# Taking the transposition of the first normalisation off TensorE: four square transposes on VectorE and sixteen on-chip transfers, one tile ahead

## The chip, the cores and the metric

The kernel runs on one core of one Trainium2 chip. The metric is the device time in microseconds (us); less is better. Every engine has a queue of its own: TensorE (PE, matrix products), VectorE (DVE), ScalarE (ACT), GpSimd (POOL), and SyncE (SP), which here issues all the transfers (DMAs). An engine works through its instructions in order, and waits on semaphores that others raise.

## What is computed

One decoder layer in fp32 on x of shape (4, 1024, 512), with a context of (4, 64, 512) and an integer mask:

```python
x = x + self_attention(layernorm(x))             # one head, causal inside blocks of 128 rows
x = x + cross_attention(layernorm(x), context)   # 16 heads of 32, 64 keys, silu instead of softmax
x = x + ffn(layernorm(x))                        # 512 -> 2048 (gelu) -> 512

qkv = z @ W_qkv; scores = blk(q) @ blk(k).T * 512**-0.5; p = softmax(causal(scores))
out = (p @ blk(v)) @ W_out.T + b_out
attn = silu(where(mask == 0, -1e9, q @ k.T * 32**-0.5)); out = (attn @ v) @ Wo.T
```

## The kernel before

The 4096 rows of x are taken as eight tiles of 512 rows (`TILES`), each four blocks of 128 rows (`NB`). An activation `z` of a tile is held twice over: in rows (`zn`, 128 rows on the partitions, 512 features along them), and transposed (`zT`, features on the partitions in four chunks of 128, `EC`, and the 512 rows of the tile along them), since TensorE contracts over partitions. To keep fp32 accuracy on a faster format, each operand is split into a high and a low part (`_hi`, `_lo`); `product` (L49 to L52) makes each product out of three matmuls.

There are three stages, each a block of its own, between which all engines wait for each other:

1. **Setup** (L279 to L423). The weights come in as 32 pieces of 256 KB (`CHUNKS`) through eight buffers `raw(n)`, which lie in `resid`; SP reloads a buffer once `split_lo` says that it is used. ACT makes the high part of each (`split_high`, L303), DVE the low part (`split_low`, L331). PE folds W_q W_k^T into `wqk` and W_v W_out into `wvo` (`fold`, 48 matmuls each, behind nine warm-up matmuls on zeros, L402), and projects the values of the four batches, which DVE takes over with their bias (L366). DVE also makes the statistics and the rows `zn` of tile 0; PE transposes them with 16 matmuls against the identity (`transposed_chunks`, L163).
2. **Attention** (L484 to about L1030). `pipeline` runs a step for each tile a: `step(0, None, 0)`, `step(1, 0, 1)`, then two steps to a loop pass, and `last_step`. A step does the self-attention of tile a and, interleaved with it, the cross-attention of tile b = a - 1. The order within it is written out by hand, for each engine. On PE: four query products (`queries`, 48 matmuls), the 16 transposes of `zn` for tile a (L163) into four PSUM banks, cross scores of heads 0 to 7 (`cross_scores`, L871 and L873, 8 matmuls), `y` = `wqk` z (48 matmuls), values, self scores (L922, L924), and so on up to the transposes for the second normalisation (L146) and the last share of the output projection.
3. **Feed-forward** (about L1035 to L1230), where PE alternates between the two products of a tile. The transposed rows of the next tile are made there by DVE alone, with 16 instructions on squares of 32x32 (L1173) for each tile.

Around the change, on DVE at the start of a step, `start_step` aggregates the statistics of tile a (L722), then makes `kb_lo` (L730, four instructions, waiting for ACT's `kb_hi`) and the rows `zn` of tile a (L140, four). For b = 0 the rows come before `kb_lo`. Then come `q_low` (L703, two for each of four chunks), `chunk_low` (L172, the low part of `zT`, four), the mask (L734), `values_low` (L740, four), and `mask_scores` (L711) for heads 0 to 7. On ACT: `keys_high` (L605), `q_high` (L610), `chunk_high` (L168, the high part of `zT`). The statistics of tile a + 1 are taken in step a from `x_in` (`next_stats`, L248), which SP loads (L240) after the first residual has used its former rows.

```python
for i in range(NB):                                             # L163, transposed_chunks
    last = pe.transpose(bank[first_bank + c][:, cols(i)], zn[:, i, cols(c)], ident[:, :])
...
pe.wait_ge(z1T_lo, EC * a + m + 1)                              # in the step, before product (m, 0)
```

## Time and profile before

| | |
|---|---|
| median of 3 runs | 1264.19 us (1264.07 to 1264.53) |
| the profiled execution's own time | 1264.23 us |
| its span | 1261.8 us |
| PE busy | 1249.1 us, 99% of the span |
| DVE busy | 662.7 us, 53% |
| ACT busy | 487.2 us, 39% |
| POOL busy | 243.7 us, 19% |
| TensorE clock granted | full speed in all 40 slices |
| setup, attention, feed-forward begin on PE at | 1.73, 43.17, 561.87 us |

The span is what the profiler records between the first and the last instruction; 2.4 us lie around it. A matmul is pipelined: it is listed with 389 ns while the next one starts 227 ns after it, so the pace is read from the starts. "Idle before <- X" names what ended the idle time in front of an instruction.

### The profile page before, as it was taken

What the parts mean: (1) busy time and instruction counts of PE and PEld (TensorE: products, weight loads), DVE (VectorE), ACT (ScalarE), POOL (GpSimd) and SP (SyncE); (2) the same over time, 40 slices, a digit from 0 to 9 for tenths busy, and PEclk for the clock granted to TensorE, in tenths of its full rate; (3) what the DMA queues carried; (4) which work ended last, traced back from release to release, by engine and by line L of the source; (5) the groups of instructions that cost most, each with busy time, mean ns of one, the idle gap of its engine ahead of it and who ended that gap; (6) DMA issues with size and microseconds to landing.
All of it is one profiled execution on the core that took longest, in us unless ns stands there. A gap on an engine that the chain in (4) does not pass through costs nothing.

```text
span 1261.8 us, 15612 instructions
## 1 busy us (share of the span) xinstructions
PE 1249.1 (99%) x5785; PEld 1040.3 (82%) x5785; DVE 662.7 (53%) x1210; ACT 487.2 (39%) x888; POOL 243.7 (19%) x225
## 2 busy tenths in 40 slices
PE   9989999999999999999999999999999999999998
PEld 7878888888888888878888888888888888888887
DVE  7476868686868686865733333434424333434211
ACT  6246555555555555564322232222222322223221
POOL 2303232323232323258502001001001010010000
PEclk9999999999999999999999999999999999999999
DMA  8220202020202020316110010010100100100000
GB/s 296 88 63 13 76 14 75 13 76 12 75 12 75 12 75 12 125 46 220 52 67 1 1 67 1 1 66 0 51 15 0 66 0 0 66 0 0 34 1 34
DMA packets 40486, 60.04 MB, mean 48 GB/s; under 512 B 4224, under 2 KB 14464, under 8 KB 40448
## 3 DMA queue, kind: packets, MB, share of 16 engines
q1 hardware_dynamic: 40448, 59.53, 14.2%
q8 instruction: 24, 0.39, 0.1%
q14 instruction: 14, 0.11, 0.0%
HBM read 41.17 MB, written 18.35 MB: 47 GB/s over the span
## 4 chain that ended last, share of the span: by engine, by line
PE 55%; DVE 0%; issue 0%; DVEq 0%
PE bank L50 18%; PE bank L52 18%; PE bank L51 18%; DVE resid L1186 0%; DVEq L1185 0%
## 5 line engine op out<-in xcount | busy, mean ns | idle before, releaser
L1176 DVE TENSOR_TENSOR hid_lo<-gelu_out,hid_hi 128x512 fp32r<-128x512 f32 x128 | 97.5, 762 | 405.8 <-ACT gelu_out L1140 405.8
L50 PE MATMUL bank<-zT,w_parts 128*128 128x512 f32 x768 | 299.1, 389 | 3.4 <-DVE zT L155 1.8
L52 PE MATMUL bank<-zT,w_parts 128*128 128x512 f32 x768 | 298.8, 389 | 0.0
L51 PE MATMUL bank<-zT,w_parts 128*128 128x512 f32 x768 | 298.8, 389 | 0.0
L1136 ACT ACTIVATE hid_hi<-bank,small 128x512 fp32r<-128x512 f32 x128 | 88.3, 690 | 498.8 <-PE bank L52 498.8
L50 PE MATMUL bank<-w2p_hi,hid_lo 128*128 128x512 f32 x512 | 199.2, 389 | 0.0
L51 PE MATMUL bank<-w2p_lo,hid_hi 128*128 128x512 f32 x512 | 199.2, 389 | 0.0
L52 PE MATMUL bank<-w2p_hi,hid_hi 128*128 128x512 f32 x512 | 199.2, 389 | 0.0
L50 PEld LDWEIGHTS bank<-zT,w_parts 128*128 128x128 f32 x768 | 144.2, 188 | 34.4 <-issue 2.3
L51 PEld LDWEIGHTS bank<-zT,w_parts 128*128 128x128 f32 x768 | 144.2, 188 | 29.9
L52 PEld LDWEIGHTS bank<-zT,w_parts 128*128 128x128 f32 x768 | 144.1, 188 | 29.8
L554 POOL TENSOR_TENSOR attn_lo<-act_in,attn_hi 128x512 fp32r<-128x512 f32 x64 | 81.6, 1296 | 225.2 <-ACT act_in L599 225.2
L52 PEld LDWEIGHTS bank<-w2p_hi,hid_hi 128*128 128x128 f32 x512 | 96.2, 188 | 20.0
L51 PEld LDWEIGHTS bank<-w2p_lo,hid_hi 128*128 128x128 f32 x512 | 96.0, 188 | 20.0
L50 PEld LDWEIGHTS bank<-w2p_hi,hid_lo 128*128 128x128 f32 x512 | 96.1, 188 | 19.9
L133 POOL TENSOR_SCALAR ve<-mv 128x4 f32<-128x4 f32 x24 | 5.8, 240 | 500.4 <-DVE mv L128 351.0
L1140 ACT ACTIVATE gelu_out<-bank,small 128x512 f32<-128x512 f32 x128 | 87.3, 682 | 0.0
L1173 DVE STREAM_TRANSPOSE z_cols<-zn 32x512 f32<-32x512 f32 x112 | 78.7, 703 | 4.2
L1100 POOL TENSOR_TENSOR resid<-resid,b_row 128x512 f32<-128x512 f32 x32 | 45.2, 1442 | 116.2 <-DVE zn L140 116.2
L691 DVE TENSOR_TENSOR yv_lo<-bank,yv_hi 128x512 fp32r<-128x512 f32 x64 | 42.6, 686 | 39.2 <-ACT yv_hi L586 30.3
L598 ACT ACTIVATE attn_hi<-act_in 128x512 fp32r<-128x512 f32 x64 | 40.0, 625 | 31.4 <-DVE act_in L711 30.6
L50 PE MATMUL bank<-w_parts,zT 128*128 128x512 f32 x128 | 51.2, 400 | 0.0
(142 smaller groups left out, 1808.8 us busy)
## 6 DMA issues: line engine op xcount, KB each, us to landing
x_in<-in_x SPq DMA_DIRECT2D x32, 256.0 KB, 3.5
x_dram<-resid SPq DMA_DIRECT2D x32, 256.0 KB, 2.1
w_raw<-in_w SPq DMA_DIRECT2D x32, 256.0 KB, 3.3
resid<-x_dram SPq DMA_DIRECT2D x32, 256.0 KB, 3.8
out_dram<-resid SPq DMA_DIRECT2D x32, 256.0 KB, 2.1
resid<-in_wqkvT SPq DMA_DIRECT2D x12, 256.0 KB, 5.2
mask_i<-in_mask SPq DMA_DIRECT2D x16, 128.0 KB, 2.7
values_now<-values_dram SPq DMA_DIRECT2D x8, 256.0 KB, 2.8
```

What stands on the lines that cost most here:

```text
L50: pe.matmul(out_ap, lhs[1], rhs[0], start=start, stop=False)
L51: pe.matmul(out_ap, lhs[0], rhs[1], start=False, stop=False)
L52: return pe.matmul(out_ap, lhs[0], rhs[0], start=False, stop=stop)
L133: pool.tensor_scalar(ve[:, :], mv[:, :, 1], LN_EPS, None, ALU.add).then_inc(ln[2], 1)
L554: pool.tensor_tensor(attn[1][:, j % 4, :], act_in[:, j % 3, :], f(attn[0][:, j % 4, :]), ALU.subtract).then_inc(attn_lo, 1)
L598: act.activation(attn[0][:, j % 4, :], act_in[:, j % 3, :], ACT.Silu)
L691: dve.tensor_tensor(hl[1][:, m, :], bank[from_bank][:, :], f(hl[0][:, m, :]), ALU.subtract).then_inc(made, 1)
L1100: pool.tensor_tensor(resid[:, slot, i, :], resid[:, slot, i, :], b2_row[:, :], ALU.add).then_inc(x2_biased, 1)
L1136: act.activation(hid[0][:, c % 4, :], bank[4 + c % 3][:, :], ACT.Gelu, bias=b1_col[:, c:c + 1])
L1140: act.activation(gelu_out[:, c % 2, :], bank[4 + c % 3][:, :], ACT.Gelu, bias=b1_col[:, c:c + 1]).then_inc(hid_full, 1)
L1173: dve.transpose(*squares(TURNS_AT_ONCE * (c - FIRST_TURN) + n)).then_inc(z3_turned, 1)
L1176: dve.tensor_tensor(hid[1][:, c % 4, :], gelu_out[:, c % 2, :], f(hid[0][:, c % 4, :]), ALU.subtract).then_inc(hid_lo, 1)
```

## The change

For the tiles 1 to 7 the rows of the first normalisation are made and transposed one step earlier, with no work on PE:

- SP loads x of tile a + 2 in step a into `ahead`, which lies in the memory of the raw feed-forward weights (`raws`); tile 1 is loaded in the setup, behind `x_in` and ahead of four small loads and the weight pieces 12 and on. DVE takes its statistics there (`stats_ahead`, `aggregate`).
- At the start of step a, DVE makes the rows of tile a + 1 (`rows_ahead`), and later in the step transposes them with four instructions on 128 partitions (`turn`), which turn each 32x32 square in its place, into the same memory.
- SP then moves the squares between the four groups of 32 partitions with sixteen DMAs of 64 KB into a new buffer `z1_cols`, and waits for them before it loads tile a + 2.
- In step a + 1 ACT and DVE make the high and low parts of `zT` from `z1_cols` (`z1_high`, `z1_low`) in place of the PSUM banks, the first of them ahead of the fourth query chunk. PE no longer transposes there; its `y` products go to banks 0 to 3, and the other banks are dealt out anew.
- In the setup, `fold` runs the high-by-high matmuls of a piece before the others, waiting only for the high parts; one warm-up matmul fewer, and the first memset is halved. DVE gets the statistics of tile 1 ahead of the values (L366 before).
- GpSimd adds the bias to `x_in` before it does its low parts, and makes the reciprocal deviation of tile a + 2 at the end of step a.

```diff
@@ setup, sync @@
                                 for i in range(NB):
                                     load_x(sp, 0, i)
+                                load_ahead(sp, 1)
@@ setup, vector @@
                         for n in range(20, WO_CHUNK):
                             split_low(n)
+                        stats_ahead(dve, 1, range(NB))
+                        aggregate(dve, 1, mv1, ln1)
                         dve.wait_ge(bias_loaded, 64)
@@ setup, tensor: fold @@
+                                pe.wait_ge(split_hi, n + 2)
+                                for m in range(EC):
+                                    pe.matmul(bank[banks + m][:, :], part[0][:, n % PARTS, cols(m)],
+                                              part[0][:, (n + 1) % PARTS, :], start=c == 0, stop=False)
                                 pe.wait_ge(split_lo, n + 2)
...
@@ attention, sync @@
+                            if more(a):
+                                sp.wait_ge(z1_turned, NB * (a + 1))
...
+                                    sp.wait_ge(z1T_lo, EC * (a + 1))
+                                for r in range(QUADS):
+                                    for q in range(QUADS):
+                                        sp.dma_start(
+                                            z1_cols[cols(q, SQUARE), :, :].rearrange(
+                                                "f c (r n) -> f c r n", r=QUADS)[:, :, r, :],
+                                            raws[cols(r, SQUARE), 0:NB, :].rearrange(
+                                                "f c (q n) -> f c q n", q=QUADS)[:, :, q, :]
+                                            ).then_inc(z1_moved, 16)
+                            if twice_more(a):
+                                sp.wait_ge(z1_moved, MOVES * (a + 1))
+                                load_ahead(sp, a + 2)
@@ attention, scalar @@
-                                for m in range(EC):
+                                for m in range(EC - 1):
                                     q_high(b, m)
-                                for c in range(EC):
-                                    chunk_high(act, a, c, 4)
+                                act.wait_ge(z1_moved, MOVES * a)
+                                act.wait_ge(q_done, EC * (b + 1))
+                                z1_high(0)
+                                q_high(b, EC - 1)
+                                for c in range(1, EC):
+                                    z1_high(c)
@@ attention, vector @@
+                        def rows_ahead(n, b):
+                            if b is not None:
+                                dve.wait_ge(z2T_done, NB * (b + 1))
+                            norm_rows(dve, lambda i: ahead[i], mv1, rstd1, ln1, n)
+                            dve.wait_ge(z1_ready, NB * (n + 1))
...
+                                    dve.transpose(turned[:, :, i, :], zn[:, i, :].rearrange(
+                                        "p (b f) -> p b f", f=SQUARE)).then_inc(z1_turned, 1)
...
-                                start_step(b, mv1, rstd1, ln1, a)
-                                for m in range(EC):
-                                    q_low(b, m)
-                                for c in range(EC):
-                                    chunk_low(dve, a, c, 4)
+                                start_step(b)
+                                if more(a):
+                                    rows_ahead(a + 1, b)
+                                q_low(b, 0)
+                                q_low(b, 1)
                                 mask_now(b)
+                                q_low(b, 2)
                                 values_low(b)
+                                z1_low(a, 0)
+                                q_low(b, EC - 1)
+                                for c in range(1, EC):
+                                    z1_low(a, c)
                                 dve.wait_ge(mask_ready, b + 1)
-                                for j in range(4):
+                                for j in range(3):
                                     mask_scores(b, j)
+                                turn(a, range(2))
+                                mask_scores(b, 3)
...
+                            turn(a, range(2, NB))
@@ attention, tensor @@
                                 queries(b, range(EC))
-                                transposed_chunks(pe, a, 4)
+                                if not first(b):
+                                    pe.wait_ge(x2_ready, NB * b)
                                 pe.wait_ge(kv_ready, len(BLOCKS) * b + HEADS_PER_CHUNK)
                                 for m in range(2):
-                                    pe.wait_ge(q_lo, 2 * (EC * b + 2 * m + 2))
+                                    pe.wait_ge(q_lo, 2 * (EC * b + m + 1))
                                     cross_scores(m)
...
-                                if c == 0:
-                                    pe.wait_ge(z1T_lo, EC * a + m + 1)
+                                if m == 0:
+                                    pe.wait_ge(z1T_lo, EC * a + c + 1)
+                                if c == 0 and b is not None:
+                                    pe.wait_ge(q_lo, 2 * (EC * b + m + 1))
```

Two places show how the order of the work moves. The first is VectorE at the end of the setup, up to its branch into the attention stage; the first fence is the kernel before, the second the change.

```order
L172 TENSOR_TENSOR zT<-bank,zT 128x512 x4
L331 TENSOR_TENSOR attn_lo<-resid,attn_hi 128x512 x4
L331 TENSOR_TENSOR w_parts<-resid,w_parts 128x512 x4
L366 TENSOR_TENSOR w_raw<-bank,bv_row 128x512 x4
L279 UNCONDITIONAL_BRANCH
```

```order
L174 TENSOR_TENSOR zT<-bank,zT 128x512 x4
L374 TENSOR_TENSOR attn_lo<-resid,attn_hi 128x512 x4
L374 TENSOR_TENSOR w_parts<-resid,w_parts 128x512 x4
L275 BN_STATS stats<-raws 128x6 x4
L281 BN_AGGR mv<-stats 128x2 x4
L411 TENSOR_TENSOR z_cols<-bank,bv_row 128x512 x4
L319 UNCONDITIONAL_BRANCH
```

Eight instructions come in between the last low parts of the weights and the four additions that end DVE's setup.

The second is VectorE at the start of step 1 (`step(1, 0, 1)`), from the aggregation on, before and in the change.

```order
L722 BN_AGGR mv<-stats 128x2 x4
L140 TENSOR_SCALAR zn<-x_in,mv,rstd 128x512 x4
L730 TENSOR_TENSOR kb_lo<-keys_now,kb_hi 32x4x64 x4
...
L172 TENSOR_TENSOR zT<-bank,zT 128x512 x4
L734 TENSOR_SCALAR mask_i<-mask_i 128x512
L740 TENSOR_TENSOR vb_lo<-values_now,vb_hi 64x4x32 x4
L711 SCALAR_TENSOR_TENSOR act_in<-bank,mask_i 128x512 x4
L691 TENSOR_TENSOR yv_lo<-bank,yv_hi 128x512 x4
```

```order
L281 BN_AGGR mv<-stats 128x2 x4
L801 TENSOR_TENSOR kb_lo<-keys_now,kb_hi 32x4x64 x4
L142 TENSOR_SCALAR zn<-raws,mv,rstd 128x512 x4
...
L829 TENSOR_TENSOR vb_lo<-values_now,vb_hi 64x4x32 x4
L805 TENSOR_TENSOR zT<-z_cols,zT 128x512
L783 SCALAR_TENSOR_TENSOR qo_hi<-bank,bias_cols,qo_hi 64x512
L783 SCALAR_TENSOR_TENSOR qo_lo<-bank,bias_cols,qo_lo 64x512
L805 TENSOR_TENSOR zT<-z_cols,zT 128x512 x3
L791 SCALAR_TENSOR_TENSOR act_in<-bank,mask_i 128x512 x3
L818 STREAM_TRANSPOSE raws<-zn 128x16x32 x2
L791 SCALAR_TENSOR_TENSOR act_in<-bank,mask_i 128x512
L818 STREAM_TRANSPOSE raws<-zn 128x16x32 x2
```

In step 1 the rows (`zn`) move from ahead of `kb_lo` to behind it, and the values' low parts move ahead of the first low part of `zT`; the transposes stand around the fourth `mask_scores`.

## Rows read from the trace of the kernel before

**Rows 1.** The page, busy time: us, share of the span, instructions.
```profile
PE 1249.1 (99%) x5785; PEld 1040.3 (82%) x5785; DVE 662.7 (53%) x1210; ACT 487.2 (39%) x888; POOL 243.7 (19%) x225
```

**Rows 2.** Timeline of PE, step of tile 4: start us, us, engine line, what [idle before].
```profile
274.54 0.39 PE L50 MATMUL bank<-zT,w_parts 128*128 128x512 f32 x1
...
285.43 1.91 PE L163 MATMUL bank<-ident,zn 128*128 128x128 f32 x16
287.10 0.47 PE L871 MATMUL bank<-qo_hi,kb_lo 128*128 128x512 f32 x1
287.41 0.39 PE L873 MATMUL bank<-qo_hi,kb_hi 128*128 128x512 f32 x1
```

**Rows 3.** Timeline of DVE, the same step, and the next step's statistics.
```profile
276.31 1.76 DVE L730 TENSOR_TENSOR kb_lo<-keys_now,kb_hi 32x256 fp32r<-32x256 f32 x4 [0.55 <-ACT kb_hi L605]
278.11 1.92 DVE L140 TENSOR_SCALAR zn<-x_in,mv,rstd 128x512 f32<-128x512 f32 x4
280.06 0.75 DVE L703 SCALAR_TENSOR_TENSOR qo_hi<-bank,bias_cols,qo_hi 64x512 fp32r<-64x512 f32 x1
...
284.40 0.75 DVE L703 SCALAR_TENSOR_TENSOR qo_lo<-bank,bias_cols,qo_lo 64x512 fp32r<-64x512 f32 x1
...
291.91 1.89 DVE L711 SCALAR_TENSOR_TENSOR act_in<-bank,mask_i 128x512 f32<-128x512 f32 x3
...
328.12 1.29 DVE L248 BATCH_NORM_STATS2 stats<-x_in 128x6 f32<-128x512 f32 x2
```

**Rows 4.** Timeline of ACT, the same step.
```profile
285.63 0.68 ACT L610 ACTIVATE qo_hi<-bank,bias_cols 64x512 fp32r<-64x512 f32 x1 [1.33 <-PE bank L52]
...
287.05 2.07 ACT L168 ACTIVATE zT<-bank 128x512 fp32r<-128x512 f32 x4
```

**Rows 5.** Groups of DVE: what, count | busy us, mean ns | idle before.
```profile
L1173 DVE STREAM_TRANSPOSE z_cols<-zn 32x512 f32<-32x512 f32 x112 | 78.7, 703 | 4.2
L1181 DVE TENSOR_TENSOR zT<-z_cols,zT 128x512 fp32r<-128x512 f32 x28 | 17.4, 684 | 0.0
```

**Rows 6.** Timeline of DVE in the setup.
```profile
17.03 2.47 DVE L248 BATCH_NORM_STATS2 stats<-x_in 128x6 f32<-128x512 f32 x4
19.53 0.38 DVE L351 BATCH_NORM_AGGREGATE mv<-stats 128x2 f32<-128x6 f32 x4
...
29.65 2.48 DVE L337 TENSOR_TENSOR w_parts<-bank,w_parts 128x512 fp32r<-128x512 f32 x4 [0.55 <-ACT w_parts L308]
...
42.18 0.69 DVE L366 TENSOR_TENSOR w_raw<-bank,bv_row 128x512 f32<-128x512 f32 x1 [1.04 <-PE bank L52]
```

**Rows 7.** Timeline of ACT in the setup: pieces 12 to 15.
```profile
19.09 2.66 ACT L303 ACTIVATE part_hi<-resid 128x512 fp32r<-128x512 f32 x4 [3.75 <-DMA resid<-in_wqkvT]
```

**Rows 8.** Windows: ..., PEclk, DMA share, GB/s (the last two numbers).
```profile
18.00:20.00 2.00, 2.00 (x10) 1.64 (x11) 1.97 (x8) 0.86 (x2) 0.00 (x0) 1.00 1.05 399
```

**Rows 9.** Timeline of PE: the first matmul of the attention stage.
```profile
43.17 0.47 PE L50 MATMUL bank<-zT,w_parts 128*128 128x512 f32 x1 [1.04 <-PEq L279]
```

**Rows 10.** Timeline of DVE, step 1.
```profile
90.30 1.76 DVE L730 TENSOR_TENSOR kb_lo<-keys_now,kb_hi 32x256 fp32r<-32x256 f32 x4 [1.33 <-ACT kb_hi L605]
...
101.00 0.41 DVE L734 TENSOR_SCALAR mask_i<-mask_i 128x512 f32<-128x512 int32 x1
101.34 1.23 DVE L740 TENSOR_TENSOR vb_lo<-values_now,vb_hi 64x128 fp32r<-64x128 f32 x4
```

**Rows 11.** Timeline of PE, step 1.
```profile
94.83 1.91 PE L163 MATMUL bank<-ident,zn 128*128 128x128 f32 x16
...
99.66 0.39 PE L50 MATMUL bank<-zT,w_parts 128*128 128x512 f32 x1
```

**Rows 12.** The page, DMA issues: what, count, KB each, us to landing.
```profile
x_in<-in_x SPq DMA_DIRECT2D x32, 256.0 KB, 3.5
x_dram<-resid SPq DMA_DIRECT2D x32, 256.0 KB, 2.1
```

**Rows 13.** Timeline of SP, the next step: two mask loads.
```profile
318.87 1.16 SPq L499 DMA_DIRECT2D mask_i<-in_mask  x2
```

More of the change, by code:

```diff
@@ L22 @@
 MASKED = -3.0e38
-WARM_UP = 9
+WARM_UP = 8
 STAGES = 3
@@ L199, in second_residual, with squares @@
                               ).then_inc(x2_ready, 1)
+        QUADS = P // SQUARE
+        TURNS = QUADS * QUADS
+        def squares(n, to):
+            row, col = divmod(n, QUADS)
+            taken = zn[cols(row, SQUARE), :, :].rearrange("p i (c q f) -> p i c q f", c=EC, q=QUADS)
+            put = to[cols(col, SQUARE), :, :].rearrange("p c (i q t) -> p i c q t", i=NB, q=QUADS)
+            return put[:, :, :, row, :], taken[:, :, :, col, :]
         layer = ExitStack()
@@ L229, in decoder_layer_program, with by_quads, by_blocks @@
             values_stored, wo_lo = sem("values_stored"), sem("wo_lo")
-            values = [w2_raw[:, b, :] for b in range(STAGES)]
-            values.append(w1_raw[:, 0, :, :].rearrange("p c n -> p (c n)"))
+            z1_cols = sb("z1_cols", [P, EC, TILE])
+            values = [z1_cols[:, b, :] for b in range(BATCH)]
+            ahead = [raws[:, i, :] for i in range(NB)]
+            turned = raws[:, 0:NB, :].rearrange("p n e -> p (n e)").rearrange(
+                "p (c q i t) -> p (c q) i t", c=EC, q=QUADS, i=NB)
+            ahead_loaded, z1_turned = [sem(f"ahead_loaded{i}") for i in range(NB)], sem("z1_turned")
+            z1_moved = sem("z1_moved")
+            MOVES = 16 * QUADS * QUADS
+            def by_quads(c):
+                return z1_cols[:, c, :].rearrange("p (r i t) -> p i r t", r=QUADS, i=NB)
+            def by_blocks(part_, c):
+                return part_[:, c, :].rearrange("p (i r t) -> p i r t", r=QUADS, i=NB)
             RAWS = 2 * NB
@@ L240, in load_x, with load_ahead, stats_ahead, aggregate @@
                 sp.dma_start(x_in[:, i, :], x_blocks[t * NB + i, :, :]).then_inc(x_loaded[i], 16)
+            def load_ahead(sp, n):
+                for i in range(NB):
+                    sp.dma_start(ahead[i], x_blocks[n * NB + i, :, :]).then_inc(ahead_loaded[i], 16)
+            def stats_ahead(dve, n, blocks):
+                for i in blocks:
+                    dve.wait_ge(ahead_loaded[i], 16 * n)
+                dve.nop(nofuse=True)
+                for i in blocks:
+                    dve.bn_stats(stats1[:, i, :], ahead[i]).then_inc(ln1[0], 1)
+            def aggregate(dve, n, mv, ln):
+                dve.wait_ge(ln1[0], NB * (n + 1))
+                dve.nop(nofuse=True)
+                for i in range(NB):
+                    dve.bn_aggr(mv[:, i, :], stats1[:, i, :]).then_inc(ln[1], 1)
             def next_stats(dve, t, blocks):
@@ L492, in first, with more, twice_more @@
                     return isinstance(t, int) and t == 0
+                def more(a):
+                    return not (isinstance(a, int) and a == TILES - 1)
+                def twice_more(a):
+                    return not (isinstance(a, int) and a >= TILES - 2)
                 with nc.Block() as block:
@@ L566, in step @@
                             if b is not None:
-                                for j in range(4, 8):
+                                for j in range(8):
                                     silu_low(b, j)
@@ L585, in y_high @@
                             act.wait_ge(y_done, EC * a + m + 1)
-                            act.activation(yv[0][:, m, :], bank[4 + m][:, :], ACT.Copy).then_inc(y_hi, 1)
+                            act.activation(yv[0][:, m, :], bank[m][:, :], ACT.Copy).then_inc(y_hi, 1)
                         def v_high(a, i):
@@ L611, in q_high, with z1_high @@
                                                bias=bq_col[r, m:m + 1]).then_inc(q_hi, 1)
+                        def z1_high(c):
+                            act.activation(by_blocks(zT[0], c), by_quads(c), ACT.Copy).then_inc(z1T_hi, 1)
                         def step(a, b, par):
@@ L640, in step @@
                             act.wait_ge(pT_done, a + 1)
-                            act.activation(probT[0][:, :], bank[1][:, :], ACT.Copy).then_inc(pT_hi, 1)
+                            act.activation(probT[0][:, :], bank[PROB_BANK][:, :], ACT.Copy).then_inc(pT_hi, 1)
                             if b is not None:
@@ L811, in step @@
                                 dve.bn_aggr(mv2[:, i, :], stats[:, i, :]).then_inc(ln2[1], 1)
-                            next_stats(dve, a + 1, (0, 1))
+                            if twice_more(a):
+                                stats_ahead(dve, a + 2, (0, 1))
+                            elif not more(a):
+                                next_stats(dve, TILES, (0, 1))
                             norm_rows(dve, lambda i: x1_rows(i, par), mv2, rstd2, ln2, a)
@@ L892, in queries @@
                             for m in chunks_:
-                                if m == 1 and not first(b):
-                                    pe.wait_ge(x2_ready, NB * b)
+                                if m < 2 and not first(b):
+                                    pe.wait_ge(x2_ready, NB * b - 2 + m)
                                 project(m, lambda c: at(wq, c, cols(m)), lambda c: at(zT, c), q_done)
@@ L941, in step @@
                             for i in range(NB):
-                                last = pe.transpose(bank[1][:, cols(i)], prob[:, i, :], ident[:, :])
+                                last = pe.transpose(bank[PROB_BANK][:, cols(i)], prob[:, i, :], ident[:, :])
                             last.then_inc(pT_done, 1)
```

118 lines of the change are left out of this document (64 added, 54 removed).

## The prediction

> **What bounds the kernel now.** I read the busy times first: PE is busy for 1249.1 of 1261.8 us, twice as long as DVE, and nothing else comes near [rows 1]. A PE that is 99% busy can be shortened in two ways only, by giving it less work or by closing the few gaps it has; and anything that makes it wait costs in full. So the timeline of PE comes next, for one step of the attention stage. The 48 query matmuls start at 274.54 and the transposes behind them at 285.43: 10.89 us / 48 = 0.227 us each, and there is no idle time between them and what follows [rows 2]. The reader is to see that a matmul removed here is time removed, and that the next engine to look at is the one that feeds PE. That is DVE in the steady steps [rows 3], ACT beside it [rows 4], and, in the setup, DVE again: its last instruction starts at 42.18 and ends at 42.87 [rows 6], and PE starts the attention stage at 43.17 after 1.04 us of waiting for the end of the block [rows 9]. The setup ends with DVE, not with PE.
>
> **Term 1, the transposes off PE.** In a steady step they take from 285.43 to 287.10, 1.67 us, and the first matmul after them takes 0.31 us to the next start (287.10 to 287.41) where 0.23 is the pace, 0.08 us more [rows 2]: 1.75 us. The listed 1.91 us is the modelled end of a pipelined group and isn't used. The removal counts for tiles 1 to 7; tile 0 keeps its transposes in the setup. For the steady steps, tiles 2 to 7: 6 x 1.75 = **10.5 us less**, if the low and high parts of `zT` are there in time.
>
> **Are they?** Walk the step from the same origin. DVE has `kb_lo` done at 278.1 and then, as before, four rows instructions (now of the next tile) to 280.0, `q_low` 0 and 1 from 280.06 as before, the mask (in the gap ahead of `q_low` 2), and `q_low` 2, whose second half ends at 284.40 + 0.75 = 285.15 [rows 3]. Then the new order: the values' low parts, 1.23 us [rows 10], to 286.4; the first `z1_low`, 0.69 us (the subtraction out of `z_cols` in the feed-forward stage has the same shape, 684 ns [rows 5]), to 287.1. ACT's `z1_high` 0 takes 0.5 to 0.6 us (four such take 2.07 us) from 285.63 on, when the fourth query chunk is done [rows 4], and is ready before DVE wants it. PE wants it after eight cross-score matmuls: 285.43 + 8 x 0.227 = 287.25. So it is met with **0.15 us to spare**. The fourth `q_low` then ends at 288.7 for 287.25 + 9 x 0.227 = 289.3, and `z1_low` 1 at 289.4 for 290.0, one chunk every 0.6 us after that against 0.68 us of PE. All are met, narrowly. The three `mask_scores` end at 292.3; before, they ended at 291.91 + 1.89 = 293.8 [rows 3], since PE was 1.67 us later. The four `turn` come in two pairs; I take 0.70 us for each, from the 32x512 transposes [rows 5], 2.8 us in all. DVE had idle time there, waiting for POOL and for ACT, and is back ahead of the four `y` low parts. Cost of the turns: nothing, while a turn stays under about 1.3 us (the fourth `mask_scores` then holds ACT's `silu`, and ACT's `y` parts behind it, and PE's self scores wait).
>
> **Are the moves?** The turns end near S = 295.6. SP issues 16 DMAs: at the 0.58 us of a mask load [rows 13] 9.3 us. A store of 256 KB lands after 2.1 us and a load after 3.5 us [rows 12]; the moves carry 64 KB each. So they have landed by 295.6 + 9.3 + 3.5 = 308.4 at the latest; four loads of x on top, 2.3 + 3.5 us, give 314.2. The statistics want them at 328.12 - 1.75 = 326.4 [rows 3], the squares are wanted only in the next step. Twelve us to spare: cost nothing. The mask load behind them on SP is issued at 318.87 [rows 13], later than that. POOL's bias additions move to where POOL idles.
>
> **Term 2, step 1.** There `kb_lo` starts at 90.30, after ACT, which waits for the keys from memory [rows 10]. The rows of a tile stood ahead of it and cost nothing; now they stand behind it. So: `kb_lo` to 92.06, rows (1.92 us) to 94.0, `q_low` 0 and 1 (1.56 us each) to 97.15, the mask 0.34 (101.00 to 101.34 [rows 10]) to 97.5, `q_low` 2 to 99.05, the values 1.23 to 100.3, `z1_low` 0 to 101.0. PE is done with the queries at 94.83 and starts `y` at 99.66 now [rows 11]; it will start at 101.0. Instead of a gain this step has a **loss of 1.35 us**. The bounds are a gain of 1.75, if DVE were early, and a loss of 3, if it were later by the rows' whole 1.92 us once more.
>
> **Term 3, the setup.** Two things lengthen DVE's chain. The statistics of tile 1 and their aggregation stand between the last low parts and the values: 2.47 + 0.38 = 2.85 us, as those of tile 0 take [rows 6]. And four more loads, 1 MB, are issued ahead of weight pieces 12 to 15. The DMA engines are at their limit there (share 1.05, 399 GB/s [rows 8]), and ACT already waits 3.75 us for piece 12 [rows 7]; 1.05 MB at 390 GB/s are 2.7 us that the piece comes later. DVE has two gaps left behind that, 0.55 and 1.04 us, both of them waits that the delay swallows [rows 6]. Sum: 2.85 + 2.7 - 0.55 - 1.04 = 3.96, **4.0 us more**. Bounds: 1.8 us if the loads find room (2.85 - 1.04), 4.8 us if the delay is 3.5 us, as of a whole load [rows 12]. PE itself has less to lose: `fold` starts its high-by-high matmuls some 0.7 us earlier, and they bridge most of the late pieces; but that is hidden, since the block ends with DVE.
>
> **Sum.** -10.5 + 1.35 + 4.0 = -5.15 us against the profiled execution's 1264.23 us: **1259.1 us**. That execution lies 0.04 us above the median of the runs, so nothing is to be corrected. The feed-forward stage and the last step keep their work.
>
> **A rule against it.** DVE's instruction turns squares of 32x32 each in its place, and sixteen transfers do what PE's bank does on the way. The Trainium skill, in "VectorE: DVE Perf Modes", section "Rules for kernel authors", says to transpose 128x128 on TensorE where PSUM can take it. That would hold if PE had time; rows 1 say that it has none and DVE has half its span, so the sum is as above. By "DMA: Bandwidth & Descriptors", section "Bandwidth", transfers under 64 KB are ruled by their descriptors, and a DMA has a fixed cost of some 2.0 us; taken one after the other the sixteen would need an estimated 34 us with it, and the sum would turn to a loss. No row here shows a DMA that waits for the one before it.
>
> **The rivals.**
> - *The setup has room.* The loads of tile 1 don't delay piece 12, or the DMA delay falls into DVE's slack, and step 1 loses nothing. Speaks for it: the whole saving is plain in rows 2. Against it: rows 7 and 8. It gives -10.5 + 0 + 1.8 = -8.7, **1255.5 us**.
> - *The margin is missed.* The first `z1_low` has 0.15 us to spare, and the strided reads of `z1_cols` or the register waits in the loop can eat that. Every steady step then waits, by 0.3 to 1.0 us, on DVE: 6 x 0.3 to 1.0 = 2 to 6 us given back, 1261 to 1265 us, **1262.5 us** in the middle.
> - *The moves don't fit (slower).* If the sixteen DMAs came down one after the other at the 2.1 us of a small store [rows 12], they would take 34 us from 295.6, and the reload 5.8 us more: 335.4, where the statistics want x at 326.4. DVE would wait 9.0 us in each step that reloads, ahead of the rows for the second normalisation, and PE, with some 1.5 us in hand, 7.5 us. Five or six such steps: +40 us, about **1300 us**. It decides from (326.4 - 5.8 - 295.6) / 16 = 1.6 us for each DMA on. For it speaks only that no row shows sixteen DMAs at once between parts of the on-chip memory; against it, that SP issues one DMA every 0.58 us [rows 13] where each takes 2.1 us or more to land [rows 12], so that several are on their way at once.
> - *The wide turn is dear (slower).* All shown transposes have 32 partitions. At four times 0.70 us for 128 the self scores would wait some 6 us in each step. Elsewhere 64 and 128 rows cost the same (0.75 us in `q_low`, 0.69 in `z_low`), so I give it little.
> - *The matmuls don't go.* The order of the changed kernel shows no transposes between queries and cross scores, so this is out.
>
> **How the numbers follow.** Chances: forecast 0.60, room in the setup 0.15, margin missed 0.17, moves 0.05, wide turn 0.03. The forecast's own range is 1257 to 1261. The range of 8 in 10 reaches down to 1254.8, which takes in the first rival, and up to 1262.6, the middle of the second. A measurement of this kernel can tell 0.2%, 2.5 us, from no change; below 1261.7 us it is faster. Of the second rival nearly half lies below that line: faster 0.60 + 0.15 + 0.07 = 0.82, same 0.10, slower 0.08.
>
> **What would show it.** PE's attention stage starts near 47.1 instead of 43.17, with a wait for the block's end of 3 us or more. ACT's piece 12 starts near 21.8. In step 1 PE waits some 3 us for `zT` between cross scores and `y`. From then on each step is 1.75 us shorter than before, with no wait on PE. The turns take 0.70 us. The moves have landed within 13 us of the last turn. Wrong would be: a repeated wait of PE for DVE's `zT` (margin), for `y` or `prob` (turns), or of DVE for the loaded rows (moves); or an attention stage that starts before 45 (setup).

## Result: slower by 0.34%, and the profile after

The changed kernel takes 1268.66 us (median of 6, 1266.68 to 1270.16), the kernel before 1264.13 us (median of 6, 1263.66 to 1264.53): ratio 1.0034, 95% interval 1.0023 to 1.0044. The forecast was 1259.1 us, at least 1254.8 and at most 1262.6. Sign and range are both missed. A second set of executions of the same changed kernel is the first experiment. The experiments ran on three other chips, where the kernel before took 1263.91 to 1264.09 us in the median, so that the times can be set side by side; each ratio is against the kernel before on the same chip.

The profiled execution took 1266.68 us with a span of 1264.9. Its busy times, against [rows 1]:

```profile
PE 1241.5 (98%) x5672; PEld 1028.8 (81%) x5672; DVE 690.7 (55%) x1238; ACT 489.6 (39%) x888; POOL 245.6 (19%) x226
```

By these rows PE is busy for 7.6 us less and still ends 3.1 us later, so about 11 us of new idle time have to be found. From the timelines of PE, with the first matmul of `y` as the mark of each step:

| stretch | before, us | changed, us | difference | forecast |
|---|---|---|---|---|
| start of the attention stage | 43.17 | 46.41 | +3.24 | +3.96 |
| from there to `y` of step 1 | 56.49 | 58.58 | +2.09 | +1.35 |
| `y` of step 1 to `y` of step 2 | 63.12 | 64.10 | +0.98 | -1.75 |
| to `y` of step 6 (four steps) | 252.50 | 248.51 | -3.99 | -7.00 |
| to `y` of step 7 | 63.15 | 63.78 | +0.63 | -1.75 |
| from there to the end of the span | 783.37 | 783.52 | +0.15 | 0 |

The differences add up to 3.10 us, the whole difference of the spans. The two losses came roughly as forecast; the gain did not: 2.4 us instead of 10.5. The timeline of PE in the changed kernel says where it waits (step 1, steps 2 to 6, then the two waits ahead of step 7's `y`; the number in brackets is the idle time before the row, and who ended it):

```profile
46.41 0.47 PE L51 MATMUL bank<-zT,w_parts 128*128 128x512 f32 x1 [3.29 <-PEq L319]
...
104.99 0.50 PE L51 MATMUL bank<-zT,w_parts 128*128 128x512 f32 x1 [3.28 <-DVE zT L805]
...
106.81 0.63 PE L51 MATMUL bank<-zT,w_parts 128*128 128x512 f32 x1
107.24 0.63 PE L52 MATMUL bank<-zT,w_parts 128*128 128x512 f32 x1
...
169.09 0.50 PE L51 MATMUL bank<-zT,w_parts 128*128 128x512 f32 x1 [0.82 <-DVE zT L805]
...
231.24 0.50 PE L51 MATMUL bank<-zT,w_parts 128*128 128x512 f32 x1 [0.46 <-DVE zT L805]
...
293.45 0.50 PE L51 MATMUL bank<-zT,w_parts 128*128 128x512 f32 x1 [0.56 <-DVE zT L805]
...
464.30 0.66 PE L148 MATMUL bank<-ident,zn 128*128 128x128 f32 x4 [0.76 <-DVE zn L142]
...
468.56 0.49 PE L51 MATMUL bank<-zT,w_parts 128*128 128x512 f32 x1 [0.85 <-DVE zT L157]
```

A repeated wait for DVE's `zT`: this is what the prediction named as the sign of the missed margin. The listed 0.4 to 0.8 us understate it, because the group before ends by a modelled 0.39 us where the pace is 0.227, and the first matmul behind a wait takes 0.11 us more to the next start; a listed 0.5 us costs about 0.75 us of a step (62.13 us in the mean of the four, against 61.38 us where nothing waits, as an experiment below shows). Behind the 3.28 us wait the starts of the matmuls are 0.43 us apart instead of 0.227 (106.81 to 107.24). The windows there, with the granted clock as the third number from the end:

```profile
104.00:106.00 2.00, 1.01 (x4) 0.86 (x5) 1.91 (x4) 0.17 (x1) 0.00 (x0) 1.00 0.45 102
106.00:108.00 2.00, 2.00 (x6) 1.59 (x5) 1.97 (x4) 0.00 (x0) 0.00 (x0) 0.52 0.32 94
108.00:110.00 2.00, 2.00 (x7) 1.53 (x6) 1.97 (x4) 0.82 (x2) 0.00 (x0) 0.63 0.00 0
```

For some 3.4 us, from 106.08 on, PE was granted the lower of its two clocks, half the full one, and lost 1.7 us.

Now the step of tile 4, the one that the prediction walked ([rows 3] are its rows before). DVE and, under it, POOL:

```profile
281.78 1.77 DVE L801 TENSOR_TENSOR kb_lo<-keys_now,kb_hi 32x256 fp32r<-32x256 f32 x4 [0.25 <-ACT kb_hi L678]
283.58 1.92 DVE L142 TENSOR_SCALAR zn<-raws,mv,rstd 128x512 f32<-128x512 f32 x4
285.72 0.74 DVE L783 SCALAR_TENSOR_TENSOR qo_hi<-bank,bias_cols,qo_hi 64x512 fp32r<-64x512 f32 x1 [0.23 <-DVE zn L142]
...
288.85 0.98 DVE L823 TENSOR_SCALAR mask_i<-mask_i 128x512 f32<-128x512 int32 x1
...
291.43 1.24 DVE L829 TENSOR_TENSOR vb_lo<-values_now,vb_hi 64x128 fp32r<-64x128 f32 x4
292.70 0.69 DVE L805 TENSOR_TENSOR zT<-z_cols,zT 128x512 fp32r<-128x512 f32 x1
```
```profile
285.75 5.23 POOL L635 TENSOR_TENSOR x_in<-x_in,bout_row 128x512 f32<-128x512 f32 x4 [3.29 <-DVE zn L142]
```

The mask takes 0.98 us and not 0.41 [rows 10], and 0.23 us pass behind `zn` where 0.03 passed before: `rows_ahead` ends with a wait of DVE for its own rows (`z1_ready`). All the mask's time lies inside POOL's bias additions, which the change puts at the start of the step. The `q_low` instructions between 285.72 and 288.85, which read the bank, keep their 0.75 us beside the same additions. The mask is stretched so in six of its eight executions (0.89 to 1.25 us); the last two, with no additions beside them, take 0.43. In the step of tile 7, which has no next tile to normalise, the additions don't wait for `z1_ready` and start earlier, and DVE's `zn` for the second normalisation of tile 6 meets them:

```profile
458.46 5.78 DVE L142 TENSOR_SCALAR zn<-resid,mv,rstd 128x512 f32<-128x512 f32 x4 [1.54 <-POOL rstd L137]
```
```profile
458.40 5.56 POOL L635 TENSOR_TENSOR x_in<-x_in,bout_row 128x512 f32<-128x512 f32 x4
```

Four rows instructions in 5.78 us instead of 1.92: those are the waits at 464 and 468. Not every instruction of DVE is held up: in step 0 four `turn` (48.43 to 50.92) run wholly beside the additions (48.40 to 53.44) and take 2.49 us, 0.62 each.

### The profile page after: what moved, and what is told of

Its sections match the earlier page's. It is cut to its first block, busy times and chain, and to the rows that moved or that the text cites. A ratio compares the mean times of both kernels' runs of the same rounds, so it can differ in the third digit from the quotient of the medians.

```text
span 1264.9 us, 15569 instructions
## 1 busy us (share of the span) xinstructions
PE 1241.5 (98%) x5672; PEld 1028.8 (81%) x5672; DVE 690.7 (55%) x1238; ACT 489.6 (39%) x888; POOL 245.6 (19%) x226
## 4 chain that ended last, share of the span: by engine, by line
PE 55%; DVE 0%; issue 0%; DVEq 0%
PE bank L51 18%; PE bank L53 18%; PE bank L52 18%; DVE resid L1289 0%; DVEq L1288 0%
```

## The experiments

Theory A: POOL's additions and DVE's instructions on on-chip memory hold each other up (the mask, `zn`), and this with the self-wait of 0.23 us makes `zT` late in every step. Rival B: the order alone is too tight, whatever POOL does. Rival C: the sixteen moves disturb DVE or PE. Apart from these: the clock behind the long waits, and the setup.

**The changed kernel again.** No edit.

> The changed kernel unchanged, as the yardstick of this chip. Its six runs spread from 1266.68 to 1270.16 us with mean granted clocks of 0.999 to 0.995; the profiled one (1266.68) has one stretch at the lower clock, 106 to 109.4 us, right behind a wait of 3.28 us. Theory of the clock: the slower runs have one or two more such stretches, behind the 3.29 us wait at the end of the setup or in step 1, each about 2 to 3 us; a profile at 1269 would show a second stretch and no new wait. Rival: the slower runs wait longer for something (a DMA), and the clock average is only an effect of it; then a profile shows a longer wait.

1269.01 us (4 runs), ratio 1.0043 (1.0028 to 1.0058). The result stands. The profiled execution was the fastest again (1267.19), so what the slower ones hold stays open here. It shows no second stretch at the lower clock, but a longer one, 6.8 us from 102.95 on, with all waits as before: `y` of step 1 to that of step 2 took 64.83 us instead of 64.10.

**Additions back between POOL's `silu_low` parts.**

```diff
-    if more(a):
-        pool.wait_ge(z1_ready, NB * (a + 2))
+    if b is not None:
+        for j in range(4):
+            silu_low(b, j)
     for i in range(NB):
...
     if b is not None:
-        for j in range(8):
+        for j in range(4, 8):
             silu_low(b, j)
```

> Only GpSimd's bias additions go back behind its first four low parts, as in the kernel before. Theory (GpSimd's additions hold up VectorE's instructions that work between parts of the on-chip memory alone): the mask instruction takes 0.42 us in every step where it takes 0.9 to 1.0, the four rows instructions at 458 us take 1.9 us where they took 5.8, PE's waits for zT in steps 2 to 7 (0.38 to 0.82 us) vanish or fall under 0.1, and so do the 0.76 and 0.85 us at 464 and 468. In all 5 to 7 us less than the changed kernel in the same clock. Rival (the first low part of zT is late of itself, by the strided reads of the moved squares and by the wait behind the rows): the mask is faster, but the waits for zT stay within 0.2 us of what they were, and only the 2 us at 464 go.

1262.78 us (11 runs), ratio 0.9987 (0.9978 to 0.9996): 5.9 us less than the changed kernel. DVE in the same step:

```profile
289.30 0.43 DVE L824 TENSOR_SCALAR mask_i<-mask_i 128x512 f32<-128x512 int32 x1
...
292.59 0.69 DVE L806 TENSOR_TENSOR zT<-z_cols,zT 128x512 fp32r<-128x512 f32 x1
```

The mask is back at 0.43 us, the waits at 464 and 468 are gone, and the steps are 61.6 us. A step in which nothing waits takes 61.38; the rest is the margin itself. `zT` is done at 292.59 + 0.69 = 293.28, and PE, whose cross scores start at 291.38, wants it at 291.38 + 8 x 0.227 = 293.20: 0.08 us late without POOL's help. In step 0, which has no `silu_low`, the additions now wait for nothing and lie beside DVE's rows of tile 1, which take 5.83 us at 46.19; PE has no wait from it in that step.

**The values' low parts behind the low parts of `zT`**, additions left where the change has them.

```diff
-    values_low(b)
     z1_low(a, 0)
     q_low(b, EC - 1)
     for c in range(1, EC): z1_low(a, c)
+    values_low(b)
```

> Only the values' low parts (1.24 us on VectorE) go from ahead of the first low part of zT to behind the fourth. GpSimd's additions stay where the change put them, so the mask still takes 0.9 us. Theory (the steady wait is the first low part of zT coming 0.5 to 0.7 us behind PE's demand, and nothing behind it): the waits for zT in steps 2 to 7 vanish, the y products of two steps follow each other by 61.4 us instead of 62.1, and that of step 1 shrinks by 1.2 us; about 5 to 6 us less than the changed kernel. The 2.1 us around 464 us stay. Rival (the waits come from the moved squares, loaded late, or from ACT's high parts): they stay.

1263.04 us (10 runs), ratio 0.9987 (0.9978 to 0.9997). Steps of 61.4 us with the mask still at 0.98: with 1.24 us taken out of DVE's way, the mask and the self-wait no longer reach PE. DVE now even waits 0.39 us for ACT's high part ahead of the first low part of `zT` (at 290.35). One step of 63.68 us stays, with the waits at 464 and 468. So it is not one cause but a sum: A and B each hold a part.

**Both together.**

> GpSimd's bias additions back between its silu low parts, and the values' low parts behind the low parts of the new zT: the two edits that each took away part of the repeated waits, together. If the port contention and the narrow margin are separate causes, the gains add: no wait of TensorE for zT in steps 2 to 7, none at 464 and 468, every step 61.36 to 61.42 us from y to y (alone, the first edit gave 61.6 and the second 61.4 with one step of 63.7). Against the first edit alone (1262.8) that is 6 x 0.2 = 1.3 us less: 1261.5 us. If both edits cure the same thing, the time stays at 1262.8 to 1263.0. The setup (start near 46.4) and the wait of step 1 (some 2 to 3 us, with the lower clock behind it) stay.

1258.48 us (5 runs), ratio 0.9954 (0.9940 to 0.9968); all steps from step 2 on are 61.38 to 61.41 us. `zT` now has 0.26 us to spare: it is done at 290.03 + 0.69 = 290.72, and PE starts `y` on time behind its eight cross-score matmuls. More cannot be won on DVE, which waits 0.95 us for ACT's high part ahead of it; that part starts only when PE has done the fourth query product.

```profile
290.03 0.69 DVE L806 TENSOR_TENSOR zT<-z_cols,zT 128x512 fp32r<-128x512 f32 x1 [0.95 <-ACT zT L688]
```
```profile
290.75 0.39 PE L983 MATMUL bank<-qo_lo,kb_hi 128*128 128x512 f32 x1
290.98 0.39 PE L51 MATMUL bank<-zT,w_parts 128*128 128x512 f32 x1
```

The expectation was 3 us too high. It left out step 1, where the values behind shorten the wait to 1.54 us, and behind that the clock stayed at 1.00 (`y` of step 1 to that of step 2: 61.51 us). Behind the wait at the end of the setup the lower clock was still granted, for 6.8 us from 46.07 on, in the profiled execution, the slowest of the five (1260.35).

**Step 1: the rows ahead of `kb_lo`**, as before the change.

```diff
+    if first(b): rows_ahead(a + 1, b)
     start_step(b)
-    if more(a): rows_ahead(a + 1, b)
+    if more(a) and not first(b): rows_ahead(a + 1, b)
```

> Only in step 1, the rows of tile 2 are made ahead of kb_lo, in VectorE's idle time there. Theory of step 1 (VectorE's chain behind the keys is too long by the rows): PE starts the y products of tile 1 about 2.6 us earlier relative to the start of the stage (56.0 us behind it, where the changed kernel has 58.6), the waits 0.76 and 0.32 us go and the one of 3.28 falls to about 2.4. Theory of the clock: with 2.4 us of waiting the clock may hold, which gives 1.7 us more; total 2.6 to 4.3 us less. Rival: the wait is set by something else (the loaded squares); then it stays at 3.3 us.

1268.02 us (5 runs), ratio 1.0034 (1.0021 to 1.0047): nothing. The rows are hidden now, but the additions wait for nothing but those rows, and run beside `kb_lo`:

```profile
94.82 4.72 DVE L801 TENSOR_TENSOR kb_lo<-keys_now,kb_hi 32x256 fp32r<-32x256 f32 x4 [1.28 <-ACT kb_hi L678]
```
```profile
93.62 5.64 POOL L635 TENSOR_TENSOR x_in<-x_in,bout_row 128x512 f32<-128x512 f32 x4 [2.11 <-DVE zn L142]
```

`kb_lo` takes 4.72 us instead of 1.76. The same collision has only found another victim.

**Additions back and rows ahead of `kb_lo`.**

> Bias additions back, and in step 1 the rows of tile 2 ahead of the keys' low parts. Alone the second edit brought nothing (1268.0), and the theory says: only because GpSimd's additions then ran beside kb_lo and stretched it from 1.76 to 4.72 us. With the additions away, kb_lo should take 1.76 us again and the rows be hidden by the wait for the keys: y of step 1 comes 1.9 to 3.3 us earlier than with the additions alone put back, with little wait left and so no lower clock there: 1262.8 - 2.6 = 1260.2 us. If kb_lo keeps over 4 us, something else than the additions stretched it and the time stays at 1262.8.

1260.95 us (8 runs), ratio 0.9973 (0.9963 to 0.9984); 1.8 us less than with the additions alone put back. `kb_lo` is at 1.76 us again, so the additions were what stretched it. From the start of `kb_lo` to `y` it is now 9.20 us instead of 10.98, the rows' time less. Most of that comes out of PE's two waits for `q_low` ahead of the cross scores (0.84 and 0.31 us, gone here) and little out of the wait for `zT`, which is 2.67 us instead of 2.81, and the clock falls behind it (0.76, 0.50, 0.89 in 104 to 110). So 1.8 of the forecast 2.6 us.

**The gap of step 1 filled** with 14 matmuls on data that nothing uses.

```diff
+    if first(b):
+        for _ in range(14):
+            pe.matmul(bank[0][:, :], kb_hi[:, 0, :], qo[0][:, 0, :],
+                      start=True, stop=True)
```

> Only 14 matmuls on idle data are added on PE in step 1, ahead of the y products, where PE waits 3.28 us; their result is never used. They take 14 x 0.227 = 3.2 us, within the wait. Theory (the gap drops the granted clock from 2.4 to 1.2 GHz for about 3.3 us): no matmul spacing of 0.427 us behind them, granted clock 1.00 in every window, about 1.6 us less than the changed kernel's profiled run, though work was added. Rival (the clock's drop has nothing to do with the gap, or costs nothing, the DVE chain being the limit there): time unchanged or longer by up to 0.3 us, spacing 0.427 still there.

1266.22 us (10 runs), ratio 1.0017 (1.0008 to 1.0026): 2.4 us less than the changed kernel, with 14 matmuls more. The windows, where the changed kernel had 0.52 and 0.63:

```profile
106.00:108.00 2.00, 1.93 (x9) 1.30 (x8) 1.90 (x4) 0.46 (x1) 0.00 (x0) 1.00 0.24 62
108.00:110.00 2.00, 2.00 (x11) 1.64 (x10) 1.94 (x3) 0.00 (x0) 0.00 (x0) 1.00 0.48 134
```

`y` of step 1 to that of step 2 took 62.46 us instead of 64.10, so the lower clock was a cost of its own, 1.6 us on top of the wait in these two profiles. The clock was not 1.00 in every window, as expected: this profile, of the slowest of the ten executions (1267.23), has 6.8 us at the lower clock around the end of the setup (from 44.84 on), and `y` of step 1 came 61.18 us behind the start of the stage instead of 58.58.

**No moves.** This kernel leaves out the sixteen transfers and the waits for them, so the transposed rows are not put together.

> The sixteen DMAs between partitions and the waits on them are left out, so that zT of the tiles 1 to 7 is made from whatever lies in the buffer; all else stays. Theory (the moves are hidden, landed 12 us ahead of their next use): every step has the same length within 0.1 us, time within 1 us of the changed kernel's in the same clock. Rival (the moves cost something: SP's later loads, or their traffic slows VectorE's or ACT's accesses): steps shorter by 0.3 us or more, or the first instructions of zT's parts faster than 0.69 and 0.63 us.

1268.07 us (5 runs), ratio 1.0035 (1.0021 to 1.0049), from `y` to `y` of steps 1 to 7 64.08, 62.11, 62.19, 62.15, 62.01 and 63.84 us, each within 0.1 us of those with the moves. Rival C is out.

**Setup: the loads of tile 1 issued behind the last weight piece.**

```diff
-    load_ahead(sp, 1)      # ahead of pieces 12 to 15
+    if n == VALUES_CHUNK + 2 * EC - 1: load_ahead(sp, 1)
```

> Only the four loads of tile 1 are issued behind weight piece 23 of the setup instead of ahead of piece 12. Theory of the setup (two additive terms on VectorE's chain: 2.1 to 2.2 us for the pieces that come later, 2.85 us for the statistics, less the gaps they swallow): ACT's pieces 12 to 15 start at 19.1 us again instead of 21.25, the stage of attention starts at 44.9 to 45.0 us instead of 46.2 to 46.4, with some 1.8 us of waiting of PE ahead of it, about 1.4 us less time. The rest is unchanged. Rival (the stage's start is set by the statistics alone, the late pieces are hidden): start stays within 0.3 us of 46.3.

1266.62 us (10 runs), ratio 1.0020 (1.0011 to 1.0030). The stage starts at 43.53 instead of 46.41: 2.88 us for the four loads, 2.7 in the forecast, twice what was expected of this edit (1.4). ACT has piece 12 at 18.37 instead of 21.25.

**Setup: the statistics of tile 1 in step 0.**

```diff
-    stats_ahead(dve, 1, range(NB)); aggregate(dve, 1, mv1, ln1)     # in the setup
+    stats_ahead(dve, 1, range(NB)); aggregate(dve, 1, mv1, ln1)     # in step 0, ahead of rows_ahead(1, None)
```
(with `norm_rstd` of tile 1 moved along on POOL)

> Only the statistics of tile 1, their aggregation and GpSimd's part go from the end of the setup to the start of step 0. Theory of the setup: the start of the stage falls from 46.3 to about 43.5 us, PE waits 0.5 to 1.0 us ahead of it, and step 0 hides the 2.85 us in VectorE's idle time ahead of the self scores; 2.8 us less time, and no stretch at the lower clock behind the setup. Rival (step 0 has no room, the y low parts come too late for the self scores): the start is earlier, but the first scores of step 0 wait for VectorE by 1 us or more and the time stays.

1264.70 us (10 runs), ratio 1.0004 (0.9994 to 1.0014). The stage starts at 44.18, behind a wait of 1.04 us instead of 3.29, and `y` of step 1 comes 58.53 us later, as before the edit (58.58): step 0 has room for them. In all it is 4.0 us less than the changed kernel where 2.8 were expected; behind the short wait no lower clock is granted at the start of the stage in this profile.

**Everything together**: additions back, values behind, rows ahead in step 1, late loads, statistics in step 0.

> All edits that a run supports: additions back, values' low parts behind, rows ahead in step 1, loads of tile 1 behind the last weight piece, statistics of tile 1 in step 0. Attention stage starts at 42.0 to 43.2 us instead of 46.4 (3.2 to 4.4 less; the wait ahead of it about 1 us, so the clock stays up), step 1 without a long wait (2.6 less), steps of 61.4 us, nothing at 464 and 468: against the two-wait version (1261.5) 3.5 + 2.6 + some 1.5 of clock less = 1253.9 us. If the setup loads of tile 1 come too late for step 0 or the statistics delay step 0's vectors, step 0 takes back 1 to 3 us: 1255 to 1257.

1252.22 us (4 runs, 1252.14 to 1252.45), ratio 0.9907 (0.9891 to 0.9922): 11.8 us faster than the kernel before. Its timeline of PE:

```profile
41.52 0.47 PE L51 MATMUL bank<-zT,w_parts 128*128 128x512 f32 x1 [1.03 <-PEq L319]
57.05 0.38 PE L1039 MATMUL bank<-zT,yv_hi 128*128 128x256 f32 x1 [1.68 <-DVE yv_lo L772]
...
98.49 0.50 PE L51 MATMUL bank<-zT,w_parts 128*128 128x512 f32 x1 [1.44 <-DVE zT L806]
```

From 98.49 on every step takes 61.38 to 61.53 us. The long waits are gone, the granted clock is 1.00 throughout, and the executions lie within 0.3 us of each other, where those of the changed kernel spread over 3.5. The wait at 57.05 is new: DVE's `zn` at 46.22 takes 5.80 us beside POOL's additions of step 0 (46.16 to 51.74), now with the statistics of tile 1 ahead of it. It is the collision that every kernel with the additions put back has in step 0. The wait suggests 1.7 us to be had at most, an estimate; no run moves these additions.

```profile
46.22 5.80 DVE L142 TENSOR_SCALAR zn<-raws,mv,rstd 128x512 f32<-128x512 f32 x4 [1.56 <-POOL rstd L137]
```
```profile
46.16 5.58 POOL L636 TENSOR_TENSOR x_in<-x_in,bout_row 128x512 f32<-128x512 f32 x4
```

## Why the prediction was wrong

**Term 1, -10.5 us: measured -2.4 us.** The removal itself is right, and exactly so: 63.13 us of a step became 61.38 where nothing waits, 1.75 us. What failed is the walk that asked whether `zT` is there in time, at three places. "The mask (in the gap ahead of `q_low` 2)" was costed at nothing and 0.34 us long, and "POOL's bias additions move to where POOL idles" at nothing. Each looks free on the timeline of its own engine, but they lie on top of each other, and the mask took 0.98 us (median of the eight 0.92, 0.43 where the additions are put back), where the gap of DVE is 0.47 us. The third is DVE's wait for its own rows (`z1_ready`), which the walk left out and the rival only grazed with "the register waits in the loop". The first `q_low` starts 5.69 us behind the step's first query matmul (285.72 - 280.03), where it was 5.52 (280.06 - 274.54). These 0.17 us are most of what turns the 0.15 us to spare into 0.08 us too late; no run takes this wait out alone. The mask adds some 0.5 us. In numbers, by the table: four steps lost 0.75 us each (3.0), of which putting the additions back gave 0.52 and the values behind the rest; step 1 to 2 lost 1.0 us to the wait and 1.7 to the clock; step 6 to 7 lost 2.4, nearly all to `zn` beside the additions. Together 8.1 us of the 10.5 forecast.

The rival "the margin is missed" had the place and the price right (0.3 to 1.0 us in each steady step, DVE's `zT`; 0.75 measured), at a chance of 0.17, but not the cause: the strided reads that it suspected take 0.69 us on DVE, as walked. A margin of 0.15 us in a walk of a dozen durations did not deserve 0.60 against 0.17. Two of its numbers don't follow either: between 1261 and 1265 us the middle is 1263 and not 1262.5, and a fifth of that range, not nearly half, lies below 1261.7, which makes the chance of "faster" 0.78 and not 0.82.

The Trainium skill, in "SBUF — State Buffer", section "Who interferes with whom", says that VectorE and GpSimd share a pair of ports to on-chip memory under an exclusive lock, which a VectorE instruction needs when it is of the fast one-source kind (`tensor_scalar`) or reads two operands there. Here the trace agrees: the mask, `zn` and `kb_lo` are stretched, to 0.98, 1.45 and 1.18 us for one (the row of four by four), from 0.43, 0.48 and 0.44, and `q_low`, with an operand in the bank, is not (0.75 beside the additions and without). That rule spoke against this change, and the prediction did not weigh it.

What the runs show by themselves is the overlap: each of the three is slow where the additions lie beside it and fast where they don't, and the `turn` instructions, with their one operand in on-chip memory, are not slowed beside them in step 0 (0.62 us each). No run shows what in the chip the two engines share.

**Turns and moves: right.** The turns take 685 ns in the mean (0.70 assumed) and nothing waits for them:

```profile
L818 DVE STREAM_TRANSPOSE raws<-zn 128x512 f32<-128x512 f32 x28 | 18.0, 685 | 0.1
```

The moves are issued in 10.41 us, 0.65 us each (9.3 us assumed for all), and land after 2.0 us in the median; the reload follows at 314.23 and nothing waits for it:

```profile
302.21 10.41 SPq L581 DMA_DIRECT2D z_cols<-raws  x16
314.23 1.92 SPq L268 DMA_DIRECT2D raws<-in_x  x4
```
```profile
z_cols<-raws SPq DMA_DIRECT2D x112, 64.0 KB, 2.0
```

They start 22.2 us behind the step's first query matmul (at 280.03); in the walk it was 21.1 (295.6 - 274.54). The slack of 12 us covers the 1.1. The reload, which waits for all sixteen, is issued 12.0 us behind their first, so at 2.0 us each they were not taken one after the other, and the landing is within 13 us, as said. That makes the rival of the serial moves wrong.

**Term 2, +1.35 us: +2.09, and a clock.** The walk had `y` at 57.83 us behind the start of the stage; it came at 58.58. 0.55 us of the 0.75 are the mask again (0.89 instead of 0.34 at 100.48), and the rest is about what the wait for `z1_ready` takes. The wait is 3.28 us, as forecast ("some 3 us"). That 3.4 us of the lower clock followed it was not in the sum: 1.7 us, which the table has in the next stretch.

**Term 3, +3.96 us: +3.24.** The mechanism is right, and the loads were sized too high. Piece 12 comes at 21.25 (21.8 forecast, 19.09 before), so DVE starts its low parts 2.09 us later and not 2.7; the statistics take their 2.87 us, and both of DVE's gaps are swallowed (0.55 and 1.04 us). 2.87 + 2.09 - 1.59 = 3.37, and DVE's last instruction ends 3.23 us later. Taken out one at a time, the loads are worth 2.88 us and the statistics 2.23, since a wait for PE of 0.48 us comes back with the second.

What the forecast missed here is on PE. With both taken out (the last experiment) the stage starts at 41.52, 1.65 us ahead of the kernel before. There the gap of 0.55 us is gone without late pieces, and the last one is 0.49 us instead of 1.04: ACT's copies of the second folded product (L308), which waited 1.12 us for PE at 29.02, wait for nothing at 27.62. The prediction called the earlier products of `fold` hidden. In the change as written they are; no run tells the setup edits apart.

DVE in the setup of the changed kernel, the wait for piece 12 and the end:

```profile
21.91 2.73 DVE L374 TENSOR_TENSOR part_lo<-resid,part_hi 128x512 fp32r<-128x512 f32 x4 [2.27 <-ACT part_hi L346]
...
40.78 2.47 DVE L275 BATCH_NORM_STATS2 stats<-raws 128x6 f32<-128x512 f32 x4
43.35 0.38 DVE L281 BATCH_NORM_AGGREGATE mv<-stats 128x2 f32<-128x6 f32 x4
43.65 2.45 DVE L411 TENSOR_TENSOR z_cols<-bank,bv_row 128x512 f32<-128x512 f32 x4
```

**The median above the profile.** The profiled execution is the fastest of the six (1266.68, mean granted clock 0.999); the slower ones, up to 1270.16, have 0.995 to 0.997. In other profiles the clock is also down behind the wait at the end of the setup (with both waits cured, 0.52 in 46 to 48). The kernel without the moves, profiled at 1267.79, has the waits of the changed kernel and one such stretch more, of 3.4 us from 45.75 on; its `y` of step 1 comes 59.82 us behind the start of the stage, 1.24 more than in the profile at 1266.68. So a part of the spread is the clock, and whether it falls there, and for how long, differs between executions. That this makes the whole spread is inferred from the mean clocks, not shown by a profile of each.

## What to carry to other kernels

An instruction that moves to where its engine idles must be laid over what the other engines do there, not only over its own: VectorE's scalings (the mask, `zn`) and the two-operand instruction out of on-chip memory (`kb_lo`) became two to three times as long beside GpSimd's additions there, while the one that reads a bank (`q_low`) and the 32x32 turns didn't. Where the next engine is busy 99% of the time, a margin of 0.15 us is no margin: put first what the bound engine wants first (here the values' low parts cost nothing a few instructions later), and only then count the gain. A change that moves work off the bound engine pays once its new chain has slack: the same idea was 0.34% slower as written and 0.93% faster with five edits to the order. A margin is read against the clock of its own step, too: times of two kernels whose steps begin 5.5 us apart can't be subtracted as they stand.

## What was not expected of the hardware

- GpSimd's addition over 128x512 (1.3 us) beside VectorE: the mask 0.43 to 0.98 us (up to 1.25), four `zn` 1.92 to 5.78 us, four `kb_lo` 1.76 to 4.72 us. The additions themselves go only from 5.02 us for four to 5.2 to 5.6.
- The granted clock went down to the lower level behind waits of PE, or already within them, for 3.4 or 6.8 us. In step 1 all nine profiled waits of 2.02 to 3.30 us were followed by it; the 2.02 us are those of the kernel with the values behind, with 0.73 and 0.30 us of waiting shortly before. At the end of the setup it was seven of ten waits of 3.27 to 3.30 us. Behind those of 1.84 us and less no profile here shows it. Fourteen matmuls that nothing uses, put into one such gap, made the kernel 2.4 us faster.
- Sixteen transfers of 64 KB within on-chip memory beside a PE that is 98% busy cost nothing that can be measured (1268.07 us without them, 1268.66 with).
